# Decoder layer, expert stage: ScalarE rounds the high parts of weights and rows, VectorE only subtracts

## The reference

```python
probs = softmax(x @ Wg + bg); keep the top 2 of 8, rescaled to sum 1
h = jnp.einsum('bsd,edf->besf', x, W1) + b1[None, :, None, :]
h = jax.nn.gelu(h, approximate=False)
y = jnp.einsum('besf,efd->besd', h, W2) + b2[None, :, None, :]
out = jnp.einsum('bse,besd->bsd', probs, y)
x = _layernorm(x + out)
```

## Time and profile before

| | us |
|---|---|
| median of three runs (lowest, highest) | 1647.21 (1641.94, 1647.63) |
| span of the profiled execution, first to last instruction | 1682.3 |
| TensorE busy in it | 1437.9 (85%) |
| VectorE busy | 1337.9 (80%) |
| ScalarE busy | 973.4 (58%) |
| GpSimd busy | 971.4 (58%) |
| first row transposes of the expert stage to its last hidden step | 1322.9 to 1615 |

### The profile page before, as it was taken

The page is one execution under the profiler, slowest core; times in us unless marked ns, Lnnn a source line. Parts: engine busy times, 40 slices in busy tenths (PEclk is TensorE's granted clock), DMA queues, the critical chain, the costliest instruction groups (busy, mean ns, idle before and its releaser), DMA issues.

```text
span 1682.3 us, 41166 instructions
## 1 busy us (share of the span) xinstructions
PE 1437.9 (85%) x10381; PEld 1230.8 (73%) x10381; DVE 1337.9 (80%) x5130; ACT 973.4 (58%) x3763; POOL 971.4 (58%) x1485
## 2 busy tenths in 40 slices
PE   4689999999999999999999999999997498988950
PEld 3478787877777777878777777778885498988840
DVE  4478988888888898888888888988876577766757
ACT  2266666666656665666666566666664255544535
POOL 2355665666666666666666666666644245544458
PEclk7599999999999999999999999999998699999975
DMA  3000000000000000000000000000000666766647
GB/s 82 11 11 7 14 18 15 15 14 13 15 15 15 15 13 13 17 14 15 13 15 13 15 14 15 13 15 16 8 11 15 189 217 208 223 191 199 203 132 214
DMA packets 89529, 95.40 MB, mean 57 GB/s; under 512 B 12137, under 2 KB 75756, under 8 KB 89282
## 3 DMA queue, kind: packets, MB, share of 16 engines
q1 hardware_dynamic: 69714, 71.97, 14.8%
q0 software_dynamic: 8896, 17.20, 3.0%
q10 hardware_dynamic: 10800, 5.06, 1.2%
HBM read 71.88 MB, written 23.35 MB: 57 GB/s over the span
## 4 chain that ended last, share of the span: by engine, by line
DVE 37%; issue 25%; ACT 15%; PE 15%; DMA 3%; another core or an unknown queue 2%; POOL 1%; DVEq 1%; SPq 1%; ACTq 0%; POOLq 0%
ACT probs L622 14%; DVE neg_max L767 7%; DVE pT L779 3%; PE ps_t L1419 3%; DVE k_pick L824 2%; DVE x1s L854 2%; PE ps_u L1419 2%; DVE turned L810 2%; DVE l_hat L871 2%; DVE yT L834 1%; PE ps_a L1381 1%; DVE top_atf L950 1%; DVE st_z L845 1%; DVE st_x L862 1%
## 5 line engine op out<-in xcount | busy, mean ns | idle before, releaser
L622 ACT ACTIVATE probs<-ps_s,neg_max 128x128 f32<-128x128 f32 x1024 | 362.6, 366 | 433.2 <-DVE neg_max L767 432.2
L508 POOL TENSOR_TENSOR probs_n<-probs,inv_sum 128x512 f32<-128x512 f32 x256 | 265.5, 1037 | 150.7 <-DVE inv_sum L773 148.6
L1265 PEld LDWEIGHTS ps_s<-kvT,u_sb 128*128 128x128 f32 x2048 | 255.3, 192 | 48.7 <-issue 44.9
L1265 PE MATMUL ps_s<-kvT,u_sb 128*128 128x128 f32 x2048 | 281.5, 281 | 3.2 <-issue 3.2
L1278 PE MATMUL ps_o<-value_w,tT 128*128 128x128 f32 x2048 | 261.8, 276 | 2.7 <-ACT tT L633 2.2
L1298 PE MATMUL ps_t<-pT,kv_rows 128*128 128x512 f32 x512 | 262.3, 594 | 0.8 <-DVE pT L779 0.8
L1278 PEld LDWEIGHTS ps_o<-value_w,tT 128*128 128x128 f32 x2048 | 244.7, 192 | 6.8 <-ACT tT L633 4.1
L570 POOL DMA_INDIRECT y_rows<-wvT,f_id x144 | 146.4, 1017 | 169.9 <-DVE wvT L1179 124.9
L520 POOL DMA_INDIRECT x_rows<-routed,pos_i x128 | 136.3, 1065 | 132.0 <-DVE pos_i L1003 100.3
L1313 PE MATMUL ps_u<-lT_hi,score_hi 128*128 128x256 f32 x512 | 184.5, 360 | 27.4 <-DVE lT_lo L893 21.1
L622 ACT ACTIVATION_READ_ACCUMULATOR probs<-ps_s,neg_max 128x1 f32 x1024 | 207.6, 203 | 0.0
(11 more groups left out here) (246 smaller groups left out, 3453.2 us busy)
## 6 DMA issues: line engine op xcount, KB each, us to landing
u_sb<-in_expert_w SPq DMA_DIRECT2D x45, 578.0 KB
tT<-in_expert_w SPq DMA_DIRECT2D x27, 578.0 KB
f_x<-x_rows SPq DMA_DIRECT2D x72, 130.0 KB
tT<-y_rows SPq DMA_DIRECT2D x32, 256.0 KB, 3.7
x_raw<-in_x SPq DMA_DIRECT2D x64, 64.0 KB, 1.8
c_raw<-in_ctx_in SPq DMA_DIRECT2D x128, 32.0 KB, 2.0
out<-u_sb ACTq DMA_DIRECT2D x16, 256.0 KB, 3.0
y_rows<-wvT,f_id POOLq DMA_INDIRECT x144
```

The source lines that it names most:

```text
L508: nc.gpsimd.tensor_tensor(probs_n[:, sl], probs[:, sl], inv_sum[:, sl, :].rearrange("p (u o) -> p u o", o=1).to_broadcast([P, UP, P]), ALU ...
L622: last = nc.scalar.activation(probs[:, sl, j], ps_s[sl][:, j * P:(j + 1) * P], ACT.Exp, bias=neg_max[:, sl, j:j + 1], accum_out=sums[:, sl ...
L1265: last = nc.tensor.matmul(ps_s[sl][:, j * P:(j + 1) * P], u_sb[:, c // 2, BT * p + b, h:h + 2].rearrange("p h s -> p (h s)"), kvT[:, c, 1 ...
```

## The change

The two masked copies (`f_x_upper`, `f_w_upper`) are gone. ScalarE now reads the raw weights and, in a new function `upper_rows`, the transposed rows in PSUM, and writes each with the output type float32r, which rounds. VectorE then subtracts that rounded value from the full one. `upper_rows(i+1)` stands behind the fourth Gelu of tile i. TensorE's work is the same, but for the count it waits for. The names list of semaphores loses `f_w_upper_done`, and is left out of the diff.

```diff
--- before.py
+++ after.py
@@ -221,9 +221,6 @@
         f_w += [u_flat[:, q * W_ROW:(q + 1) * W_ROW] for q in range(W_RING - 3)]
         f_x = sb("f_x", [P, RING, TB, ROW])
         f_id = sb("f_id", [P, RING, TB])
-        f_x_upper = wq_raw[:].rearrange("p (n t) -> p n t", t=T)[:, 0:2]
-        f_w_upper = wkT[:].rearrange("p (q c) d -> p q (c d)", q=2)
-
         f_xT_hi, f_xT_lo = (w[:].rearrange("p q l s -> p q (l s)") for w in (lT_hi, lT_lo))
         f_w1_hi, f_w1_lo = (w[:].rearrange("p (q h) d -> p q (h d)", q=H // FC)[:, 0:2] for w in (score_hi, score_lo))
         f_h = wkv_raw[:].rearrange("p (q c t) -> p q c t", q=2, t=T)
@@ -691,8 +688,16 @@
 
             def upper_weights(i, q):
 
-                act.wait_ge(f_w_upper_done, i + 1)
-                nc.scalar.activation(f_w1_hi[:, q % 2], f_w_upper[:, q % 2], ACT.Copy).then_inc(f_w1_hi_done, 1)
+                act.wait_ge(fw_in[q], (i + (W_RING - q)) * (16 // W_RING))
+                act.wait_ge(f_h_ps, count(i * (FC // 2) - FC // 2))
+                act.wait_ge(f_w1_lo_done, count(i - 1))
+                nc.scalar.activation(f_w1_hi[:, q % 2], f_w[q][:, 0:F], ACT.Copy).then_inc(f_w1_hi_done, 1)
+
+            def upper_rows(i, q):
+
+                act.wait_ge(f_xT_ps, i + 1)
+                act.wait_ge(f_h_ps, count(i * (FC // 2) - FC // 2))
+                nc.scalar.activation(f_xT_hi[:, q % 2], F_XT[q % 2], ACT.Copy).then_inc(f_x_upper_done, 1)
 
             def ffn(i, q):
                 act.wait_ge(fw_in[q], (i + (W_RING - q)) * (16 // W_RING))
@@ -704,8 +709,11 @@
                                          bias=f_w[q][:, B1_AT + c:B1_AT + c + 1]).then_inc(f_h_done, 1)
                     if c == 1 and (not isinstance(i, int) or i + 1 < NF):
                         upper_weights(i + 1, (q + 1) % W_RING)
+                if not isinstance(i, int) or i + 1 < NF:
+                    upper_rows(i + 1, (q + 1) % W_RING)
 
             upper_weights(0, 0)
+            upper_rows(0, 0)
             turns(act, NF, ffn, W_RING, W_RING)
 
             def last(g, q):
@@ -1146,24 +1154,17 @@
             nc.vector.tensor_copy(exw_i[:], exw_f[:]).then_inc(tab_ready, 1)
 
             def rowsT(i, q):
-                dve.wait_ge(f_xT_ps, i + 1)
+                dve.wait_ge(f_x_upper_done, i + 1)
                 dve.wait_ge(f_h_ps, count(i * (FC // 2) - FC // 2))
-                nc.vector.tensor_scalar(f_x_upper[:, q % 2].bitcast(I32), F_XT[q % 2].bitcast(I32), HI_BITS, None,
-                                        ALU.bitwise_and).then_inc(f_x_upper_done, 1)
-                dve.wait_ge(f_x_upper_done, i + 1)
-                nc.vector.tensor_copy(f_xT_hi[:, q % 2], f_x_upper[:, q % 2]).then_inc(f_xT_done, 1)
-                nc.vector.tensor_tensor(f_xT_lo[:, q % 2], F_XT[q % 2], f_x_upper[:, q % 2], ALU.subtract).then_inc(f_xT_done, 1)
+                nc.vector.tensor_tensor(f_xT_lo[:, q % 2], F_XT[q % 2], f_xT_hi[:, q % 2].bitcast(F32), ALU.subtract).then_inc(f_xT_done, 1)
 
             def split_weights(i, q):
 
                 dve.wait_ge(fw_in[q], (i + (W_RING - q)) * (16 // W_RING))
 
-                dve.wait_ge(f_w1_hi_done, count(i - 1))
+                dve.wait_ge(f_w1_hi_done, i + 1)
                 dve.wait_ge(f_h_ps, count(i * (FC // 2) - FC // 2))
-                nc.vector.tensor_scalar(f_w_upper[:, q % 2].bitcast(I32), f_w[q][:, 0:F].bitcast(I32), HI_BITS, None,
-                                        ALU.bitwise_and).then_inc(f_w_upper_done, 1)
-                dve.wait_ge(f_w_upper_done, i + 1)
-                nc.vector.tensor_tensor(f_w1_lo[:, q % 2], f_w[q][:, 0:F], f_w_upper[:, q % 2], ALU.subtract).then_inc(f_w1_lo_done, 1)
+                nc.vector.tensor_tensor(f_w1_lo[:, q % 2], f_w[q][:, 0:F], f_w1_hi[:, q % 2].bitcast(F32), ALU.subtract).then_inc(f_w1_lo_done, 1)
 
             def result(i, q):
                 dve.wait_ge(f_y_ps, i + 1)
@@ -1391,14 +1392,14 @@
 
             def rowsT(i, q):
                 pe.wait_ge(f_in[q % RING], (i + (RING - q % RING)) * (16 // RING))
-                pe.wait_ge(f_xT_done, count(2 * i - 2))
+                pe.wait_ge(f_xT_done, count(i - 1))
                 for b in range(TB):
                     last = nc.tensor.transpose(F_XT[q % 2][:, b * P:(b + 1) * P], f_x[:, q % RING, b, 0:D], ident[:])
                 last.then_inc(f_xT_ps, 1)
 
             def hidden(i, q):
                 pe.wait_ge(fw_in[q], (i + (W_RING - q)) * (16 // W_RING))
-                pe.wait_ge(f_xT_done, 2 * i + 2)
+                pe.wait_ge(f_xT_done, i + 1)
                 pe.wait_ge(f_w1_hi_done, i + 1)
                 pe.wait_ge(f_w1_lo_done, i + 1)
                 pe.wait_ge(f_h_done, count(i * FC - FC))
```

More of the change, by code:

```diff
@@ L285, in decoder_layer @@
         weight_done atf_done picked_done mask_done seen_done rows_kept rids_kept rank_ps pos_all_done pos_sel_done pos_f_done
-        pos_done pad_ready cnt_ps tab tab_base tab_ready f_xT_ps f_x_upper_done f_xT_done f_w_upper_done f_w1_hi_done f_w1_lo_done f_h_ps f_h_done f_y_ps f_yb_done f_id_done f_y_done
+        pos_done pad_ready cnt_ps tab tab_base tab_ready f_xT_ps f_x_upper_done f_xT_done f_w1_hi_done f_w1_lo_done f_h_ps f_h_done f_y_ps f_yb_done f_id_done f_y_done
         e_sum_done e_z_done e_stats e_moments e_eps e_rstd e_nm_done e_out_done""".split()
@@ L295, in decoder_layer @@
          rids_kept, rank_ps, pos_all_done, pos_sel_done, pos_f_done, pos_done, pad_ready, cnt_ps, tab, tab_base,
-         tab_ready, f_xT_ps, f_x_upper_done, f_xT_done, f_w_upper_done, f_w1_hi_done, f_w1_lo_done, f_h_ps, f_h_done, f_y_ps, f_yb_done, f_id_done, f_y_done, e_sum_done, e_z_done, e_stats,
+         tab_ready, f_xT_ps, f_x_upper_done, f_xT_done, f_w1_hi_done, f_w1_lo_done, f_h_ps, f_h_done, f_y_ps, f_yb_done, f_id_done, f_y_done, e_sum_done, e_z_done, e_stats,
          e_moments, e_eps, e_rstd, e_nm_done, e_out_done) = [sem(n) for n in names]
```

## The result

Beside the kernel before on the same chip the changed kernel took **1676.55 us** (median of five, 1673.6 to 1684.7) against **1647.21 us** (1641.9 to 1648.0): ratio 1.0187, 95% interval 1.016 to 1.0214, so 29 us slower. The forecast was 1672 us with a range of 1648 to 1686 and "slower" at 0.69.

The account below looks back on a forecast made before the run. TensorE was taken to bound the expert stage at 3.45 us a tile; the new 4.12 us ring adds 4 us and the stalls 21, so 1647.2 + 25 = 1672 us, range 1648 to 1686.

Parts of the forecast that it names:

- TensorE bounds the kernel before in this stage: Expert stage: TensorE's gapless 3.45 us a tile is the floor, with some stalls on top; VectorE's masks don't bind.
- The ring through ScalarE: From one hidden step to the next through Gelus, weight copy, row copy and row subtraction: six links, 4.12 us a tile.
- The row copy: Ring's fourth link, ScalarE's upper_rows, 128 x 256 out of PSUM: 0.40 us, midway between 0.29 and 0.50.
- the last link: Ring's sixth link, from the start of VectorE's row subtraction to the hidden matmul: 0.69 us.
- the short kind: Last link at its shortest, 0.55 us instead of 0.75, counted in about one tile of four.
- One sign: New trace: TensorE's hidden matmul waits for `lT_lo` in nearly all 72 tiles, about 0.7 us each.
- The relief of VectorE: VectorE loses weight mask, row mask and row copy, 1.2 us a tile, 86 us in all; costed at nothing.
- The weight hand-over: VectorE's weight subtraction now waits for ScalarE's weight copy but is done before the rows come; costed at nothing.
- The first tiles: Start of the expert stage, at a granted clock of 0.56: some 2 us more.
- The stalls and the 35 us: Ten disturbed tiles, about 21 us, staying or belonging to the recording, whose trace is 35 us longer than the median.
- The first rival: The stalls are in plain runs too and go: 1651 us, not to be told from no change; 0.24, with ring not closing.
- The clock: Rival: TensorE's pauses lower the clock, the stage doubles to near 490 us, 1840 us in all; chance 0.03.

Follow-up runs that it names:

- the first trace: The unchanged kernel before, as profiled for the prediction: span 1682.3 us, against 1645.8 us when profiled again.
- two other orders: Changed kernel with the row copy moved between the Gelu pairs, 1654.8 us; with the weight copy also moved ahead of the first Gelu, 1639.2 us.
- The version with TensorE as the only bound: Changed kernel with the weight copy ahead of the first Gelu and the row copy between the Gelu pairs: 1639.2 us, ratio to the kernel before 0.9957.
- the high level: Groups of runs in which the unchanged kernel before took 1686 to 1695 us.
- the trace with the needless copy: Kernel before plus one ScalarE copy per tile into memory nothing reads, behind the fourth Gelu: 1685.9 us, ratio 0.999.
- the rows' part alone: Kernel before with only upper_rows on ScalarE behind the fourth Gelu, weights still masked on VectorE: 1686.6 us, ratio 1.0004; again 1690.4 us, ratio 0.9973.
- the low level: Groups of runs in which the unchanged kernel before took near 1647 us.

## Why the prediction was right, point by point

- **TensorE bounds the kernel before in this stage.** Right, and more so than the first trace showed: 252 of 254 us busy.
- **The ring through ScalarE, 4.12 us.** Right in mechanism and order. Measured: 3.96 us median, 4.04 mean. The row copy took 0.398 us for 0.40. The sum was 0.08 to 0.16 too long, mostly in the last link, from the subtraction to the hidden matmul: 0.69 forecast, 0.62 and 0.55 in the tile above and the one before it. The forecast gave the short kind one tile in four; it is 0.52 to 0.56 us in 56 of 71 tiles. (0.55 was not the shortest of the first trace either, which has three of 0.52.) The experiments bear the ring out: the same work in two other orders took 22 and 37 us less (beside a kernel before of 1647), and a copy put on it added its pace to each step. One sign did not come as stated: the wait for `lT_lo` is about 0.3 us in 43 tiles, not 0.7 in nearly all.
- **The relief of VectorE, "I cost that relief at nothing".** Wrong in size. The version with TensorE as the only bound needs 247.0 us for the stage, the kernel before 254.0: at most about 7 us were to be had, and doubling one mask cost 10.5 us. In the change the ring hid this.
- **The weight hand-over, costed at nothing.** Right for the change, where the row ring is longer: VectorE ends the weights just before the rows come. It holds only there: with the rows left on VectorE the same hand-over made a step of 4.48 us.
- **The first tiles.** 2 us more forecast; their two steps took 5.90 and 6.05 us against 4.55 and 5.32, 2.1 us more.
- **The stalls and the 35 us.** The number was right, the reading was not. I took the stage of plain runs to be 269 us and put the rest on recording. It was 254 us, because the first trace came from an execution near the high level. The ten stalls at 21 us were also too small an account of what it had lost: behind its first two steps, nineteen are over 4.2 us, and they hold 30 us more than as many at the usual 3.52. The two errors, 15 us there and 8 us in the ring, work against each other: 25 us forecast, 29.3 measured, 32.7 between the two traces' stages. So the nearness of 1672 to 1676.55 is partly luck: only 4 of the 25 us came from the ring, which is the cause; the other 21 stood for a kernel before that is faster in plain runs, which was so, but neither by that much nor for that reason.
- **The first rival, "The stalls are in plain runs too, and go".** Wrong for the result, where the kernel before has no such stalls. At the high level something like it happens: ratio 0.9948, three late events in place of ten. Its mechanism is not shown. In the first trace of the kernel before, each of the ten late events came 3 to 4 us behind a slowed weight mask (16 masks took 0.56 to 0.63 us for 0.42), and so did 14 of the 15 of the trace with the needless copy. The Trainium skill ("SBUF — State Buffer", "SBUF: two separate sides") has a VectorE instruction in a two-port mode and a GpSimd instruction exclude each other for the whole instruction. The 0.61 us of L1163 agree in part: it began inside a GpSimd instruction of 0.97 us and was slowed, but it ended at 1499.81, 0.25 us behind that one's end at 1499.56, too soon to have waited for it and then run its 0.42 us (spans on GpSimd are rough). And the lock is not shown to be the whole cause: late events also came in the changed kernel, which has no L1163, the longest in a tile whose VectorE instructions all had their usual length; and the fifteenth came behind a mask of 0.43 us. Nor does the absence of L1163 alone rule the lock out: by that section of the Trainium skill it also holds between a VectorE instruction with two inputs in SBUF, as L1167 is, and a GpSimd instruction that reads SBUF. No slowing of L1167 is seen: it took 0.69 us in all 72 tiles of the kernel after.
- **The clock.** It did not fall: 1.00 with TensorE busy 93% by the rows (46.4 of 50 us).

**Still open:** what makes the kernel before take 40 us longer in one group than in another, and what delays the events. The two are not the same question: the kernel with the row mask done twice and the rows' part alone, both at the high level, have no slowed weight mask and no late event on VectorE. In two disturbed tiles, and the one above, GpSimd had just issued indirect DMAs nearly back to back; but the undisturbed tile of the kernel with the weight copy first has the same pair (GpSimd at 1452.77 and 1454.04). No experiment tested it.

## What to carry over

Moving work to an engine with much idle time can lengthen the kernel, if the work lands at the end of that engine's order for a step and the next step waits for it. Write down the ring from one step to the next, link by link, before counting busy time; here it gave the step of each version of the change within 0.2 us (it missed for VectorE's order in the kernel before: 3.98 expected with the mask done twice, 3.73 measured). The same work placed ahead of what nobody waits for yet (the weight copy first, the row copy before the second Gelu pair) turned a loss of 1.9% into a gain of 0.3 to 0.4%, both at the low level.

If the span of a trace is 2% off the median of the runs, don't put the difference down to recording; get a second trace before building on its stalls.

## What the runs showed of the hardware

- The same kernel took 1647 to 1649 us in three groups of runs and 1686 and 1695 us in two, on other chips. Between its two traces (spans 1682.3 and 1645.8) the difference lies in the one stage that mixes loads (200 to 229 GB/s in all) with GpSimd's indirect DMAs. The changed kernel, with its regular step of 4 us, took only 8 us more at the high level than at the low one (1684.8 and 1676.6); the kernel before, with 3.5 us, took 39 to 48 more.
- ScalarE writes a 128 x 256 block from PSUM as float32r in 0.40 us, what the columns say between 0.294 (128) and 0.501 (384) for float32 output.
- At the high level a weight mask on VectorE (128x512) that began inside one of GpSimd's indirect DMA instructions took 0.61 us for 0.42, and in two traces 24 of 25 late events on VectorE came 3 to 4 us behind such a mask.
- Added VectorE work made a kernel faster by 0.3% at the high level and slower by 0.7% at the low one.
